# A four-layer graph network on one core: the fourth block sum moves from GpSimd to VectorE, and the narrow blocks between the first seven-product blocks of a row are laid out anew

## The reference

```
h = relu(layernorm(x)); x = x + L0(h)   # twice: h = tanh([adj @ h, h] @ W0[k])
h = relu(layernorm(x)); x = x + adj @ (h @ W1) + bias
h = relu(layernorm(x)); x = x + adj @ (h * (u >= 0.1) / 0.9)
h = relu(layernorm(x)); x = x + [h, (adj @ h) / (rowsum(adj) + 1)] @ W3.T
```

## Time and profile before

| | |
|---|---|
| median of 3 runs | 2221.46 us (2221.43 to 2221.57) |
| the profiled execution's own time | 2219.71 us |
| its span in the trace | 2217.9 us |
| TensorE busy | 2181.0 us |
| VectorE busy | 1767.2 us |
| GpSimd busy | 289.7 us |
| ScalarE busy | 173.5 us |
| granted TensorE clock | 1.00 |

### The profile page before, as it was taken

The page is one execution under the profiler, slowest core; times in us unless marked ns, Lnnn a source line. Parts: engine busy times, 40 slices in busy tenths (PEclk is TensorE's granted clock), DMA queues, the critical chain, the costliest instruction groups (busy, mean ns, idle before and its releaser), DMA issues.

```text
span 2217.9 us, 38303 instructions
## 1 busy us (share of the span) xinstructions
PE 2181.0 (98%) x15854; PEld 1235.5 (56%) x15854; DVE 1767.2 (80%) x3200; ACT 173.5 (8%) x388; POOL 289.7 (13%) x184
## 2 busy tenths in 40 slices
PE   6999999999999999999999999999999999999999
PEld 3555555555555467777755667676344444444446
DVE  7467777777887689999767889897888877778777
ACT  1000000000002321111100000000100000000000
POOL 0000000000000124343302344453000000000000
PEclk9999999999999999999999999999999999999999
DMA  9999999999999889999999999999899999999997
GB/s 397 421 420 418 419 415 413 399 399 405 400 379 363 301 322 333 346 350 350 345 420 350 342 335 353 338 327 364 356 397 410 409 411 407 397 410 398 415 400 308
DMA packets 118765, 839.50 MB, mean 379 GB/s; under 512 B 14016, under 2 KB 16320, under 8 KB 17088
## 3 DMA queue, kind: packets, MB, share of 16 engines
q1 hardware_dynamic: 114480, 832.62, 95.3%
q10 hardware_dynamic: 3344, 2.33, 0.3%
q0 software_dynamic: 768, 2.10, 0.3%
HBM read 834.90 MB, written 2.10 MB: 377 GB/s over the span
## 4 chain that ended last, share of the span: by engine, by line
PE 91%; DVE 4%; DMA 2%; issue 1%; POOL 1%; ACT 0%; SPq 0%; DVEq 0%; POOLq 0%
PE double_acc L933 33%; PE single_acc L961 20%; PE single_acc L905 16%; PE spare L933 14%; PE spare L905 7%; DMA store<-in_adj 2%; PE natural L1025 1%; DVE store L1372 1%; POOL store L881 1%; DVE store L1373 0%; DVE stats L1169 0%; PE spare L1038 0%; DVE partial L1272 0%; DVE partial L1403 0%; DVE partial L1429 0%
## 5 line engine op out<-in xcount | busy, mean ns | idle before, releaser
L933 PE MATMUL double_acc<-store,operand 128*64 128x512 f32 x3632 | 808.9, 592 | 1.2 <-ACT operand L1137 1.2
L933 PEld LDWEIGHTS double_acc<-store,operand 128*64 128x64 f32 x3632 | 280.3, 137 | 435.2 <-issue 414.3
L961 PE MATMUL single_acc<-store 128*64 128x256 f32 x2528 | 485.2, 379 | 0.0
L961 PE MATMUL single_acc<-store,operand 128*64 128x256 f32 x1944 | 452.1, 379 | 9.8 <-POOL store L881 9.8
L905 PE MATMUL single_acc<-store,operand 128*64 128x256 f32 x3696 | 438.7, 381 | 21.3 <-DVE operand L1205 11.9
L881 POOL TENSOR_TENSOR store<-store 128x512 f32<-128x512 f32 x162 | 279.7, 1726 | 1126.5 <-DVE store L1373 1126.4
L905 PEld LDWEIGHTS single_acc<-store,operand 128*64 128x64 f32 x3696 | 293.1, 138 | 189.0 <-issue 85.0
L961 PEld LDWEIGHTS single_acc<-store 128*64 128x64 f32 x2528 | 311.5, 137 | 40.9
L933 PE MATMUL spare<-store,operand 128*64 128x512 f32 x1456 | 330.3, 592 | 0.7 <-DMA store<-in_adj 0.7
L961 PEld LDWEIGHTS single_acc<-store,operand 128*64 128x64 f32 x1944 | 263.5, 137 | 70.7 <-issue 18.2
L1272 DVE TENSOR_TENSOR partial<-spare,partial 64x256 f32<-64x256 f32 (+1 forms) x250 | 126.4, 506 | 162.5 <-PE spare L933 109.7
(11 more groups left out here) (88 smaller groups left out, 934.7 us busy)
## 6 DMA issues: line engine op xcount, KB each, us to landing
store<-in_adj SPq DMA_DIRECT2D x792, 1024.0 KB, 8.3
for_layer<-in_u POOLq DMA_DIRECT2D x16, 128.0 KB, 6.2
out_rows<-resid ACTq DMA_DIRECT2D x15, 128.0 KB, 5.9
resid<-in_x SPq DMA_DIRECT2D x2, 512.0 KB, 6.1
resid<-in_x SPq DMA_DIRECT2D x1, 1024.0 KB, 13.5
out_rows<-resid ACTq DMA_DIRECT2D x2, 64.0 KB, 1.7
w_stack<-in_w_both ACTq DMA_DIRECT2D x2, 32.0 KB, 8.7
ident<-in_identity ACTq DMA_DIRECT2D x1, 64.0 KB, 16.3
```

The source lines that it names most:

```text
L933: last = nc.tensor.matmul(acc[half_of(half), :], operand[:, b.j * TPB + t, half_of(half)], stream[:, t, :], start=b.first and t == 0, stop ...
L961: last = nc.tensor.matmul(acc[half_of(half), nodes_of(nodes)], weights[:, t, :], data[:, t, :], start=first and k in (0, 2), stop=final an ...
```

## The change

- `make_sums`: VectorE makes t4 as well, as a third instruction (128 x 512). GpSimd's step and the semaphore `second_sum_made` go.
- The plain block between the first sevens is now put by the table `ALL_SEVEN`, not by the row's length. Row 6 of sweep 2 and row 15 of sweep 3 get one (one seven less each), so there are 160 sevens and not 162.
- `BELOW_IN`: the narrow blocks (4, 4), (5, 5) and (6, 6) for sweep 4 are no longer issued after rows 5, 6 and 7 of sweep 3. They are issued in rows 9, 13 and 14 of that sweep, after the first two sevens.
- `combine` of a row whose following row has no sevens comes right after its `post`, and not after the following row's `doubles`.

```diff
+BELOW_IN = {9: 4, 13: 5, 14: 6}
-ALL_SEVEN_OVER = 8
+ALL_SEVEN = {2: range(6), 3: range(9, NB - 1)}
...
-            between = first + SEVENS_BEFORE_PLAIN if len(self.double) <= ALL_SEVEN_OVER else None
+            between = first + SEVENS_BEFORE_PLAIN if self.i not in ALL_SEVEN[self.sweep] else None
...
+        if row.sweep == 3 and row.i in BELOW_IN:
+            at[PLAIN_FIRST + SEVENS_BEFORE_PLAIN].append(lambda: late(4, BELOW_IN[row.i], [BELOW_IN[row.i]]))
...
-        if row.sweep == 3 and row.i >= 1 and row.i - 1 not in FILL_UP[4] and row.i - 1 not in TURN:
+        if row.sweep == 3 and row.i >= 1 and row.i - 1 not in (*FILL_UP[4], *TURN, *BELOW_IN.values()):
             late(4, row.i - 1, [row.i - 1])
...
         if what == "post" and (of.sweep, of.i) in columns:
-            combines.append(("combine", of))
+            (combines if of.r + 1 in of_row else steps).append(("combine", of))
...
         elif what == "doubles":
-            if of.r + 1 not in of_row or of.r not in of_row:
-                steps.extend(combines)
-                combines.clear()
             sums7(of_row.get(of.r + 1, [])[:SUMS])
...
             for what, of in PLAN:
-                if what == "sums7":
-                    n, at = SEVEN_BLOCKS.index(of), LOAD_OF[of.number].slot * SLOT
-                    _, t2, t4 = block_sums(of)
-                    wait_loaded(pool.wait_ge, of)
-                    pool.wait_ge(second_sum_made, n + 1)
-                    nc.gpsimd.tensor_tensor(t4, inside(at + 2 * BLOCK, (BLOCK, 2)), t2, ALU.subtract).then_inc(sums_made, 1)
-                elif what == "post" and 2 * NB <= of.r + 2 < 3 * NB:
+                if what == "post" and 2 * NB <= of.r + 2 < 3 * NB:
...
-                y22 = inside(at + 2 * BLOCK + HALF, (BLOCK, 2))
-                t1, t2, _ = block_sums(b)
+                y21, y22 = inside(at + 2 * BLOCK, (BLOCK, 2)), inside(at + 2 * BLOCK + HALF, (BLOCK, 2))
+                t1, t2, t4 = block_sums(b)
                 link(nc.vector.tensor_tensor(t1_t3, y12_y22, y11_y12, ALU.subtract))
-                nc.vector.tensor_tensor(t2, y22, t1, ALU.subtract).then_inc(second_sum_made, 1)
+                link(nc.vector.tensor_tensor(t2, y22, t1, ALU.subtract))
+                nc.vector.tensor_tensor(t4, y21, t2, ALU.subtract).then_inc(sums_made, 1)
```

More of the change, by code:

```diff
@@ L789, in gnn_kernel @@
         sums_made = sem("sums_made")
-        second_sum_made = sem("second_sum_made")
         first_product_saved = sem("first_product_saved")
```

## The result

| | before | changed |
|---|---|---|
| median | 2221.43 us (6 runs, 2219.64 to 2221.57) | 2209.39 us (6 runs, 2209.36 to 2209.67) |
| the profiled execution's own time | 2219.71 us | 2209.67 us |
| its span | 2217.9 us | 2207.8 us |

The ratio is 0.9948 with a 95% interval of [0.9936, 0.9961]. I had predicted 2210.5 us, in a range of 2208.5 to 2216. The medians are 12.0 us apart, the profiled executions 10.0. The other 0.3 is that the changed kernel's profiled execution was the slowest of its six. Against the lower group the change brings 10.3 us, against the upper one 12.0.

What follows compares the result with a forecast made beforehand. TensorE, busy 98% of the span, was taken as the bound, losing time to late sums. -12.05 + 0.83 + 0.1 + 0.1 = -11.0 us gives 2208.7 profiled; 1.75 more gives median 2210.5, range 2208.5 to 2216.

Steps and rivals of the forecast that it cites:

- TensorE's loss, 12.05 us, all from late sums: In sweeps 2 and 3, TensorE loses 12.05 us to late sums, the most the change can bring.
- the gap of 16.95: At a change of rows, TensorE can start the fourth seven 16.95 us after the last seven, against 18.01 before.
- t2 and t4 at 0.69, 95 us given back to VectorE: In the block sums, t2 and t4 take 0.69 us each; VectorE gains 110.4 us of work and gets 95.0 back.
- 1783 or a little under: VectorE's total busy time in us, forecast for the profile of the changed kernel.
- The rival of a slower kernel: VectorE becomes the bound in the stretches 755 to 1100 and 1185 to 1530: 34 us more, 2255; chance 0.03.
- Its threshold: VectorE becomes the bound when less than 0.21 of the 0.59 us of blocking per block comes back; free time 0.48.
- Narrow blocks moved at no cost: Moving narrow blocks in sweep 3 leaves TensorE's work and the loads the same, costing nothing.
- Two plain blocks, 0.83 us: In row 6 of sweep 2 and row 15, two sevens become plain, adding 0.83 us.
- The tight places: Row 14's post in sweep 2 and row 9 to row 8 there: 0.1 us taken for each.
- waits at 712 and at row 9 to row 8: Sweep 2 places where TensorE waiting for VectorE 0.3 us more than forecast would show the prediction wrong.
- The sum for the profiled execution: The whole kernel's profiled execution: 2219.7 - 11.0 = 2208.7 us.
- 1.75 added: Whole kernel: the median of the runs shown lies 1.75 us above the profiled execution, giving 2210.5.

Runs made afterwards that it cites:

- t4_alone: The kernel before with only t4 moved to VectorE; blocks, narrow blocks and combine stay where they were: 2212.54 us.
- narrow_back: The changed kernel with the narrow blocks (4,4), (5,5), (6,6) back after rows 5, 6 and 7 of sweep 3: 2211.80 us.
- row15_sevens: The changed kernel with transposes ahead of combine, sweep 2 row 14's combine after row 13's doubles, and sweep 3 row 15 all sevens again: 2208.89 us.
- gpsimd_beside: The changed kernel plus an extra 128 x 512 GpSimd subtraction for each seven, from a constant into a buffer nobody reads: 2248.68 us.
- row6_sevens: The changed kernel with transposes ahead of combine, sweep 2 row 14's combine after row 13's doubles, and sweep 2 row 6 all sevens again: 2208.02 us.

## Why the prediction was right, and where it was off

- **TensorE's loss, 12.05 us, all from late sums.** Right. It is all gone in the changed kernel, and the gap of 16.95 that I gave for a change of rows with t4 on VectorE and nothing between measured 16.98 to 16.99 in three kernels (t4_alone, narrow_back, row15_sevens).
- **t2 and t4 at 0.69, 95 us given back to VectorE.** Right: 0.692 each. VectorE's busy time came out at 1762.4, where I had 1783 or a little under; combine's second instruction had been held up as well (0.81 and now 0.29 each, 13.5 us in all with the two instances of another shape), which I had left out. gpsimd_beside shows the mechanism.
- **The rival of a slower kernel** is real in kind: gpsimd_beside is slower by 39 us. Its threshold was wrong, since it was an average over all rows (0.48 free per seven). gpsimd_beside stays under that average (0.42) and is slow all the same, because a long row has room for 0.43 and got 0.72.
- **Narrow blocks moved at no cost, 2.3 us gained by them.** Right (2.4 when undone).
- **Two plain blocks, 0.83 us.** The price is right. The one in row 15 buys back about twice as much (0.48 lost without it, on top of its own 0.42), the one in row 6 nothing.
- **The tight places.** This is the term that was mis-sized: 0.2 us in the sum, 0.83 measured (0.28 and 0.55). I had named waits at 712 and at row 9 to row 8 as signs of being wrong, and both are there: 0.06 and 0.33 us. The second is the larger miss, since I had `take_doubles` end just as the post wants it. I had also left out that any standstill costs TensorE another 0.22 us, "refilling" in the expectations above: the piece after it is longer (0.69 for a post of 0.47, 6.26 for a pair of sevens of 6.04).
- **The median.** 2210.5 predicted, 2209.39 measured. I had laid the profiled difference on a median, and that median belonged to the upper of two groups. The sum for the profiled execution missed by 1.0 us one way (2208.7, measured 2209.67: 0.63 in the tight places, 0.30 at the start, which is chance of that execution), the step from there to the median by 2.0 the other (1.75 added; the median is 0.28 below). The two errors partly cancel, so the prediction came out closer than its working deserved: that part is luck.

## What to carry to other kernels

When one engine waits for another at a fixed place of a loop, write the queue of the late engine from the last common event on, with its measured durations; where I did so, in sweep 3, it gave the arrival to 0.05 us and told that its rows needed cover. Where I did not follow VectorE's queue from the end of row 10 on, it missed a wait of 0.33, and it put a plain block into row 6 that row6_sevens shows to be unneeded. An instruction handed to GpSimd to relieve VectorE can cost VectorE all that it saves (here 1767.2 us busy with the offload and 1762.4 without it), and adds its own latency. In an in-order queue, put the step that waits for a third engine behind the one that doesn't.

## What the runs showed of the hardware that was not expected

- A standstill of TensorE of 2.4 us was followed, in about half of the executions, by some 3 us at the lower clock: 1.7 us on top. After one of 1.3 us at the same place this did not happen in 11 runs. Two groups of times of one kernel can be a sign of a standstill that lowers the clock in some executions only.
- VectorE and GpSimd hold each other up without a byte in common: in gpsimd_beside 0.69 becomes 1.41 us on VectorE and 1.04 becomes 1.95 on GpSimd. In the kernel before, where they share data, 0.69 becomes 1.64 and 1.27 becomes 2.1.
- A standstill of TensorE costs 0.22 us more than its length (a post of 0.47 takes 0.69, a pair of sevens of 6.04 takes 6.26).
